# Mixture of experts behind decay attention on one core: turns placed singly, half-tile jobs spread over the quarters, empty rows left out of the scatter, routing over six units

## The reference

```
x = x + attention(layernorm(x))            # linear attention with a decay scan, 16 heads
x = x + moe(layernorm(x))

moe(x):
  scores = softmax(x @ gate_w)             # 8 experts
  topk_w, topk_idx = top_k(scores, 2)
  comb = scatter of topk_w over the experts
  g = silu(x @ w_gate[e]) * (x @ w_up[e])  # 352 wide, for each expert e
  routed = sum over e of comb[e] * (g @ w_down[e])
  shared = silu(x @ sw_gate) * (x @ sw_up) @ sw_down     # 704 wide
  return routed + shared
```

## Time and profile before

| | us |
|---|---|
| three runs | 657.11, 659.87, 660.52 |
| median | 659.87 |
| the profiled execution, whole | 661.91 |
| its span, first to last instruction | 660.1 |
| TensorE busy in the span | 625.6 (95%) |
| VectorE busy | 419.8 (64%) |
| ScalarE busy | 265.0 (40%) |
| GpSimd busy | 192.3 (29%) |

### The profile page before, as it was taken

One profiled execution on the slowest core, in us unless ns is written; L12 is line 12 of the kernel. 1 busy time (PEld: TensorE's weight loads), 2 busy tenths in 40 slices (PEclk: granted clock), 3 DMA queues, 4 the chain that ended last, 5 costly groups with the idle time before them and its releaser, 6 DMA issues.

```text
span 660.1 us, 11671 instructions
## 1 busy us (share of the span) xinstructions
PE 625.6 (95%) x3785; PEld 411.8 (62%) x3786; DVE 419.8 (64%) x832; ACT 265.0 (40%) x411; POOL 192.3 (29%) x250
## 2 busy tenths in 40 slices
PE   7999999999999999989999999999999999999992
PEld 7777677677777765546665656666565556556550
DVE  5998887997998865886877876634424433323330
ACT  4464653463453445456666776321111111111110
POOL 5210131231103226002111212144455544443531
PEclk8999999999999999999999999999999999999996
DMA  6751013513425696758664824478878898985852
GB/s 224 293 171 33 16 49 98 154 43 89 129 65 150 203 239 193 199 164 170 139 177 114 181 36 70 75 130 141 112 128 121 138 127 140 132 133 96 147 84 32
DMA packets 107132, 84.76 MB, mean 128 GB/s; under 512 B 76528, under 2 KB 82672, under 8 KB 107088
## 3 DMA queue, kind: packets, MB, share of 16 engines
q1 hardware_dynamic: 85744, 43.28, 29.2%
q0 software_dynamic: 12128, 27.93, 24.8%
q10 hardware_dynamic: 9216, 12.98, 5.9%
HBM read 43.80 MB, written 22.54 MB: 100 GB/s over the span
## 4 chain that ended last, share of the span: by engine, by line
PE 53%; DMA 8%; issue 6%; DVE 6%; SPq 1%; POOL 1%; ACT 1%; POOLq 1%; ACTq 0%; DVEq 0%
PE ps_g L598 12%; PE ps_y L598 12%; PE ps_u L598 12%; PE ring L442 8%; DMA x_in<-x_job 4%; PE turn_h L649 2%; DMA x_job<-xn_scratch,job_tok 2%; PE ps_g L610 1%; PE ps_u L610 1%; PE ps_y L610 1%; PE ps_y L661 1%; DMA out_dram<-y_job,job_tok 1%; DMA out_dram<-x 1%; SPq L899 1%; DMA out_dram<-y_job,upper_tok 1%
## 5 line engine op out<-in xcount | busy, mean ns | idle before, releaser
L1285 ACT CAST hidT<-turn_h 128x384 f16<-128x384 f32 x68 | 32.4, 477 | 167.0 <-PE turn_h L649 166.4
L442 PE MATMUL ring<-xnT_h,wq_h 128*128 128x512 f32 x188 | 76.7, 408 | 2.7 <-DVE wq_l L1442 1.4
L442 PE MATMUL ring<-xnT_h,wq_l 128*128 128x512 f32 x188 | 74.4, 395 | 0.0
L442 PE MATMUL ring<-xnT_l,wq_h 128*128 128x512 f32 x188 | 74.1, 394 | 0.0
L598 PE MATMUL ps_g<-routed,x_in 128*128 x384 | 67.8, 313 | 4.4 <-DMA x_in<-x_job 4.3
L598 PE MATMUL ps_y<-routed,hidT 128*128 x288 | 69.0, 386 | 1.3 <-DVE hidT L1565 1.3
L1133 POOL DMA_INDIRECT out_dram<-y_job,job_tok x32 | 52.9, 1653 | 56.2 <-DVE y_job L1959 43.6
L598 PE MATMUL ps_g<-shared,x_in 128*128 128x384 f16 (+1 forms) x384 | 67.4, 313 | 0.0
L1580 DVE SCALAR_TENSOR_TENSOR hid<-ps_u,job_hid,silu 128x352 f32<-128x352 f32 x36 | 21.0, 584 | 72.3 <-PE ps_u L598 41.7
L598 PE MATMUL ps_y<-shared,hidT 128*128 128x512 f16 x240 | 57.1, 379 | 6.3 <-DVE hidT L1565 3.4
L598 PE MATMUL ps_u<-shared,x_in 128*128 128x384 f16 (+1 forms) x384 | 62.5, 313 | 0.0
(11 more groups left out here) (296 smaller groups left out, 1186.7 us busy)
## 6 DMA issues: line engine op xcount, KB each, us to landing
x_res<-in_L_attn_x_dram SPq DMA_DIRECT2D x20, 256.0 KB, 3.4
routed<-in_L_ffn_w_gate_dram ACTq DMA_DIRECT2D x6, 704.0 KB, 4.8
routed<-in_L_ffn_w_up_dram ACTq DMA_DIRECT2D x6, 704.0 KB, 6.9
out_dram<-x SPq DMA_DIRECT2D x16, 256.0 KB, 3.8
xn_scratch<-xn_hl SPq DMA_DIRECT2D x16, 256.0 KB, 2.5
out_dram<-y_job POOLq DMA_DIRECT2D x16, 256.0 KB
x_in<-in_L_attn_x_dram SPq DMA_DIRECT2D x12, 256.0 KB, 3.4
routed<-in_L_ffn_w_down_dram ACTq DMA_DIRECT2D x6, 512.0 KB, 7.6
```

The source lines that it names most:

```text
L442: ins = pe.matmul(ps, a, b, start=(i == 0), stop=(i == len(steps) - 1))
L1285: act.copy(hidT[:, 0], turn_h[:, 0:FC, :]).then_inc(s["hidTh_s"], 1)
```

## The change

Five things, in the order of the diff. Pair jobs become 5, 14, 23 and 32 (`SIDE` 9, one at place 5 of each). The one-hot tables begin in unit 10 and not 8. `product` calls `inside` three times, after the third, fourth and fifth matmul, and each call issues one transpose; a pair's gate product still issues all three in a row. Job 34 issues gate(35), up(35), down(34). The scatters get a bounds test (index at most 2047, no error beyond), so that rows with a spare number are not moved; a job without tokens no longer waits for the scatter before it. The place operations of unit 6 go to unit 7 and are one fewer, the job tables of unit 7 go to units 8, 9 and 11, and token tables and masks from units 24 and 25 to 26 and 27. The copies of experts stand in the first three jobs of each quarter.

```diff
-    SIDE = JOBS // 2
-    PAIR_AT = 8
-    FIRST_PAIRS = (PAIR_AT, SIDE + PAIR_AT)
+    SIDE = JOBS // PAIRS
+    PAIR_AT = 5
-    is_pair = lambda r: r % SIDE in (PAIR_AT, PAIR_AT + 1)
-    pair_of = lambda r: 2 * (r // SIDE) + r % SIDE - PAIR_AT
+    is_pair = lambda r: r % SIDE == PAIR_AT
+    pair_of = lambda r: r // SIDE
...
-        FIRST_TABLE = 4
+        FIRST_TABLE = 5
...
-                    if q == 3 and inside is not None:
-                        inside()
+                    if inside is not None and 3 <= q < 3 + FC:
+                        inside(q - 3)
                     ins = pe.matmul(ps, a[i][:, k, :], w(j, k), start=(start and q == 0),
                                     stop=(stop and q == len(steps) - 1))
...
+            def turn_chunk(u, c, first=False, shared_half=None):
+                if c == 0:
+                    pe.wait_ge(s["hid_s"], u + 1)
+                    if shared_half == 1:
+                        pe.wait_ge(s["hid_twin"], u // 2 + 1)
+                    if not first:
+                        pe.wait_ge(s["hidT_s"], u)
+                col = FCOL[c] if shared_half is None else c * P
+                ins = pe.transpose(turn_h[:, c, :], hid[:, col:col + P], ident[:, :])
+                if c == FC - 1:
+                    ins.then_inc(s["turned_h"], 1)
...
-                    if ahead == 2:
-                        up_product(u + 1, 1 - b, up_w)
+                    gate_product(u + 1, t + 1, 1 - b, gate_w, inside=lambda c: turn_chunk(u, c))
+                    up_product(u + 1, 1 - b, up_w)
                 if pair:
                     down_pair(u, t, routed_pair(r)[2])
                 else:
                     down_product(u, t, routed_unit(r)[2], True, True)
-                if ahead == 1:
-
-                    up_product(u + 1, 1 - b, up_w)
...
                     pool.indirect_dma_start(out[:, :], bass.IndirectOffsetOnAxis(job_tok[:, r:r + 1], 0),
-                                            y_job[:, b, :], None, compute_op=ALU.add).then_inc(s[f"yo{b}"], 16)
+                                            y_job[:, b, :], None, bounds_check=T - 1, oob_is_err=False, compute_op=ALU.add).then_inc(s[f"yo{b}"], 16)
...
+            def places():
+
                 link(dve.tensor_copy(slot_i[:, :], slot_f[:, :, :].rearrange("p k t -> p (k t)")))
...
-                for least, by in ((PAIR_AT, 2), (SIDE + PAIR_AT, 2), (JOBS + 2, SIDE - 2), (JOBS, PAIR_AT - JOBS)):
-                    link(dve.tensor_scalar(slot_by[:, :], slot_j[:, :], float(least), float(by), ALU.is_ge, ALU.mult))
-                    link(dve.tensor_tensor(slot_j[:, :], slot_j[:, :], slot_by[:, :], ALU.add))
...
+                link(dve.tensor_scalar(slot_ji[:, :], slot_ji[:, :], SIDE - 1 - PAIR_AT, None, ALU.add))
+                link(dve.tensor_scalar(slot_ji[:, :], slot_ji[:, :], 3, None, ALU.arith_shift_right))
+                link(dve.tensor_copy(slot_by[:, :], slot_ji[:, :]))
+                link(dve.tensor_tensor(slot_j[:, :], slot_j[:, :], slot_by[:, :], ALU.add))
+                link(dve.tensor_scalar(slot_by[:, :], slot_j[:, :], float(SIDE - 1), float(PAIR_AT - SIDE * JOBS),
+                                       ALU.mult, ALU.add))
+                link(dve.scalar_tensor_tensor(out=slot_by[:, :], in0=slot_j[:, :], scalar=float(JOBS), in1=slot_by[:, :],
+                                              op0=ALU.is_ge, op1=ALU.mult))
+                link(dve.tensor_tensor(slot_j[:, :], slot_j[:, :], slot_by[:, :], ALU.add))
...
-                       RANK_UNIT: first_slots, 6: slots, 7: job_experts,
+                       RANK_UNIT: first_slots, 6: slots, 7: places, 8: lambda: experts(job_ef, whole_no, jobs_end),
+                       9: lambda: (experts(job_el, left_no, left_end), job_experts()), 11: job_waits,
...
-                if ahead == 2:
+                if ahead >= 1:
                     hidden(HALVES * NT + r + 1, job_hid[:, bass.ds(r + 1, 1)])
                 weigh_y(r, b)
-                if ahead == 1:
-                    hidden(HALVES * NT + r + 1, job_hid[:, bass.ds(r + 1, 1)])
...
+            for side in range(PAIRS):
+                for b in range(3):
+                    job_step(SIDE * side + b, (SIDE * side + b) % 2)
+                    copy_expert(side, b)
+                for r in range(SIDE * side + 3, min(SIDE * (side + 1), JOBS - 2)):
+                    job_step(r, r % 2)
```

More of the change, by code:

```diff
@@ L606, in pair_product @@
                     if q == 3 and inside is not None:
-                        inside()
+                        for c in range(FC):
+                            inside(c)
                     for h in range(2):
@@ L637, in up_product @@
                 product(ps_u[:, 0:n], x_halves(tb), w, KC, True, True).then_inc(s["u_mm"], 1)
-            def turn_hidden(u, first=False, shared_half=None):
[L640 to L650, removed]
+            def turn_chunk(u, c, first=False, shared_half=None):
[9 more added lines that the diff above has]
+                    ins.then_inc(s["turned_h"], 1)
+            def turn_hidden(u, first=False, shared_half=None):
+                for c in range(FC):
+                    turn_chunk(u, c, first, shared_half)
             def down_product(u, t, w, start, stop, first=False, twin=False):
@@ L812, in _ @@
                     gate_w, up_w = routed_unit(0)[0:2]
-                gate_product(u + 1, t_next, t_next % 2, gate_w, inside=lambda: turn_hidden(u, shared_half=half), n=n)
+                gate_product(u + 1, t_next, t_next % 2, gate_w, inside=lambda c: turn_chunk(u, c, shared_half=half), n=n)
                 up_product(u + 1, t_next % 2, up_w, n=n)
@@ L837, in job_step @@
                     gate_w, up_w = routed_pair(r + 1)[0:2]
-                    gate_pair(u + 1, t + 1, 1 - b, gate_w, inside=lambda: turn_hidden(u))
+                    gate_pair(u + 1, t + 1, 1 - b, gate_w, inside=lambda c: turn_chunk(u, c))
                     up_pair(u + 1, 1 - b, up_w)
@@ L848, in job_step @@
                     down_product(u, t, routed_unit(r)[2], True, True)
-                if ahead == 1:
-                    up_product(u + 1, 1 - b, up_w)
             pe.wait_ge(s["split_s"], len(pieces))
[L854 to L868, removed]
+            r = 0
+            while r < JOBS:
+                alike = 0
+                while r + alike < JOBS - 1 and not is_pair(r + alike) and not is_pair(r + alike + 1):
+                    alike += 1
+                if r % 2 == 0 and alike >= 2:
+                    with pe.Fori(r // 2, (r + alike) // 2) as i:
+                        job_step(2 * i, 0)
+                        job_step(2 * i + 1, 1)
+                    r = (r + alike) // 2 * 2
+                else:
+                    job_step(r, r % 2, 2 if r < JOBS - 1 else 0, is_pair(r), r + 1 < JOBS and is_pair(r + 1))
+                    r += 1
         @block.sync
@@ L2001, in copy_expert @@
                 dve.tensor_copy(copy_done[:, d % HALVES, part], routed_done[:, e, part]).then_inc(s["copied"], 1)
-            COPY_FROM = (1, FIRST_PAIRS[0] + 2)
             dve.wait_ge(s["split_s"], len(pieces))
-            for r in range(COPY_FROM[1] + 6):
-                job_step(r, r % 2)
-                for side in range(2):
-                    at = r - COPY_FROM[side]
-                    if 0 <= at < 6:
-                        copy_expert(2 * side + at // 3, at % 3)
-            with dve.Fori((COPY_FROM[1] + 6) // 2, JOBS // 2 - 1) as i:
-                job_step(2 * i, 0)
-                job_step(2 * i + 1, 1)
+            for side in range(PAIRS):
[4 more added lines that the diff above has]
+                    job_step(r, r % 2)
             job_step(JOBS - 2, 0, ahead=1)
```

36 lines of the change are left out of this document (16 added, 20 removed).

## The result

The changed kernel took 656.22 us as the median of 10 runs, against 660.59 for 10 runs of the kernel before. The ratio is 0.9941, its 95% interval 0.9914 to 0.9968: about 3.9 us faster, where 7.6 were forecast. One of the ten runs, of 666.01 us, was in a slower state and does not count in the ratio. The time lies in the predicted range; the gain is half of what was predicted. The profiled execution took 656.56 us, its span is 654.8.

A forecast was written before the change was run, and what follows sets the result against it. TensorE was taken to bound the kernel, its idle time and slow-clocked end being winnable. Terms -2.5 - 2.4 - 3.0 + 0.3 = -7.6 us gave 654.3 on the profiled scale, 652.3 as a median; range 647.0 to 658.5.

The forecast's parts named there:

- Turns, 0: TensorE's three transposes per job, now single: each costs 0.11 us by passage, not weight load, so moving them gains 0 us.
- rival A: A turn's time is a weight load that longer products hide: 10.2 us more gained, 642.1 us; chance 0.04.
- Routing, 2.5: Units 6 to 8: small operations spread over six units end most of TensorE's waits for hidT, gaining 2.5 us.
- The last two jobs, 2.4: End of span: up(35) ahead of down(34) saves 0.9 us of gap, and 1.5 because the clock stays up.
- The bounds test, 0: GpSimd's scatter issue: the test's cost, shown by no row, stays under 2.6 us of slack, so 0 on the path.
- Switches, 0.3: Routed part: single pairs switch more often between whole and half tiles, costing 0.3 us.
- Waits for x_in, 3.0: Routed gate products: single pairs let GpSimd's queue catch up, so 3.0 of 4.3 us of waits go.
- The relief by skipped rows: DMA engines, 0.80 busy, are relieved of 468 rows and 44 in whole jobs, of 4608; part of the 3.0 us.
- Rival C: Single pairs in four places each cost half of the 4.3 us waits, 8.6 in all: 659.6 us; chance 0.10.
- The range's lower end: 647.0 us, given as all waits gone and 1.5 us for the spread of runs.

The follow-up runs named there:

- quiet profiles: Scatters move nothing (bounds test at row 0): kernel before 655.08 us, with routing alone 653.04, last two jobs alone 653.52, changed with grouped turns 651.36, changed 651.74.
- run 1: Changed kernel with its three turns in one group again: 0.9979 of the kernel before, 657.40 us.
- run 2: Changed kernel without the bounds test, so empty rows are added into the spare rows again: 0.9932 of the kernel before, 654.56 us.
- run 8: Kernel before with the bounds test alone: 0.9996 of the kernel before.
- run 3: Kernel before with only the routing's small operations spread over more units: 1.0008 of the kernel before.
- run 18: Changed kernel unaltered, timed a third time: 0.9895 of the kernel before, median 654.40 us.

## Why the prediction was right or wrong

*Turns, 0:* right, and nothing of rival A appeared. That a turn's own passage takes the 0.11 us, the rows ahead of the change had not quite shown: the load of the next product's weights could have set that spacing too. It doesn't, since in the changed kernel the routing products (line 710, 108 columns, also with float16 weights) follow each other, and are followed by a down product, 0.05 us apart. By the Trainium skill ("TensorE: Matmul & The Clock Gate", "LDWEIGHTS") the load would have set the spacing. In a group that gives the same 0.11 us; but the trace has 0.11 us behind a single turn too, which starts 0.15 us behind a product that covers its load, so it doesn't agree. That grouped turns ran 0.004 slower once was a draw of waits: with four buffers it is not there, and in the quiet profiles the routed parts agree within 0.01 us.

*Routing, 2.5:* right in place and nearly in size: 2.4 in the profile, 2.0 in the quiet median. One of the waits that should not have come did, 0.23 us in unit 11, and the one in unit 8 is 0.40 and not 0.15. The first wait of that chain, in unit 6, stayed (0.80 before, 1.13 after), and one of 0.51 at 394 us went.

*The last two jobs, 2.4:* the mechanism is right, the size was not. The sure part is one gap less, 1.05 us (21.50 against 20.45 us in quiet profiles), where 0.9 was priced. The fall of the clock, priced at 1.5, was read from one execution and taken as a rule, while it came in three of seven: with it the gain is 1.6 in the median. The 2.2 us that this stretch gained in the first pair of profiles had the fall in it (1.6) and 0.5 us of the test against it.

*The bounds test, 0:* this term was put at nothing because the issue's length seemed fixed. The length is; but 0.50 us stand ahead of each scatter that has waited, and of these the last is on the path: 0.5 us. Whether more of it reaches the path is open (runs 1, 2 and 8).

*Switches, 0.3:* 0.45 us. In the quiet profiles it is 207.43 us from the first routed gate product to the last with four single pairs and 206.98 with two double ones.

*Waits for x_in, 3.0:* this step failed, and it is the one that halved the gain: the stretch in which they stand gained 0.8 us where 2.7 were forecast. It had two halves. The first, that the double pairs cause the waits, rested on their place in one trace. But they differ from execution to execution. With the pairs in the old places four profiles have 4.3, 6.0, 6.3 and 2.1 us, in the new ones five have 2.4, 5.5, 2.3, 4.5 and 1.9, means of 4.7 and 3.3. Some of the 1.4 may be real; it is no more than these differences can tell.

The second half, that GpSimd has 2.6 us to spare for each job and so catches up, counted its issue times and left out what it waits for: gathers waited 38.3 us for the transposing DMA of two jobs back, and after the change scatters wait 14.7 us more for landings, which goes with the test and not with the pairs. A gather held up in this way can go out together with the next transposing DMA, which at job 28 then took 7.7 us (9.1 at most, in run 3). Four buffers take away that hold, and from job 6 on the waits but for 0.7 us at most; scatters that move nothing take the waits away too. That the two meet because the gather was held is argued and not shown, as transposing DMAs start beside gathers in the quiet kernels too and take at most 5.8 us there. The relief by skipped rows was the third support, and runs 2 and 8 show none. Rival C had this place and asked too much of it.

The range's lower end does not follow from its own terms: all waits gone and 1.5 us of spread give 652.3 - 1.3 - 1.5 = 649.5, not 647.0.

In sum, 3.7 us come from what the quiet kernels show, less half a us for the test. The changed kernel's three ratios (0.9941, 0.9945, 0.9895) are 4 to 7 us, with the luck of the waits in them. Open is why the waits differ so much among executions of one kernel; no run here shows that.

## What to carry to other kernels

A wait in one trace is one draw: before pricing its cause, ask whether the transfers behind it have a steady distance, and look for a term that has a place in the program (a chain of small operations, an order of products) before one that has a place only in an execution. A queue's slack is counted with what it waits for and not with its busy time alone. Where a queue is held by the buffer of a transfer in flight, look for memory that has become free: here two more buffers gained 2.3 us in the kernel before, and the waits fell by 1.4 at most with the rearranged pairs, within the noise. And an instruction's length is not its whole price: look at how long after its release it starts.

## What the runs showed of the hardware that was not expected

A transposing DMA of 128 x 1024 float16 took 2.8 us with nothing beside it (runs 1 and 2), and anything from 2.7 to 9.1 us with a gather and a scatter beside it (runs 1, 2, 3 and 18); where the scatters moved nothing, at most 5.8. An indirect scatter of a half whose rows nearly all fail the bounds test still takes 1.43 us to issue and lands after 2.5 to 3.3 us (run 8), where one that moves 64 rows lands after 3.8 to 5.2 (before). A scatter with the test at row 2047 starts 0.50 us later behind what it waited for than one without a test or with the test at row 0; one that waited for nothing starts 0.30 us behind the instruction before it in either case. The granted clock can fall after 2.0 us of idle time in two gaps (three executions of seven), or stay at 1.00 after the same two; after single waits it fell behind one of 2.37 us and not behind 2.13 and 2.64.
